# Folded transforms, the order of z's and the rows' transposes, and a split write of the output, in a fused convolution, attention and expert kernel

## The chip, the cores and the metric

The kernel runs on one core of a Trainium2 chip. The metric is the device time of one execution in microseconds (us). Before the change it was 386.15 us in the median of three runs (382.89 to 387.73).

## What is computed

The input x is 16 images of 128 channels and 16 x 16 pixels, float32. Three blocks follow each other, each with a residual sum.

```python
x = x + conv(group_norm(x))            # filters made from x itself, 7 x 7, per image and channel
t = to_tokens(x)                       # 256 tokens of 128 channels an image
q = tanh(layer_norm(t))
t = t + softmax(q q^T / sqrt(128)) layer_norm(t)
t = t + experts(layer_norm(t))         # 8 experts, hidden width 256, the best 2 of each token
```

The filters of the first block: keys are a 1 x 1 product of x to 49 channels, a softmax over the 256 pixels, a product with x (`fraw`), a 1 x 1 product, a normalisation over all 128 x 49 values, a weighting, relu, and another 1 x 1 product (`filt`). The depthwise convolution with them is done in frequency space: a real Fourier transform of side 19 (181 frequencies) written as matrix products.

## The kernel before

Two images are a pair, and there are 8 pairs. A loop of 14 rounds, unrolled in the program text, runs 7 stages over the pairs: in round i stage N works on pair i (group norm), A on pair i-1 (transposes of the normed image, keys, softmax, `fraw`), B on pair i-2 (filters, forward transform), C on pair i-3 (product of spectra, inverse transform, sum `t1`, layer norm to z), D on pair i-4 (transposes of z, tanh, scores, attention, sum `t2`, second layer norm), E on pair i-5 (normed rows, router, ranks) and F on pair i-6 (dispatch of the rows to DRAM). Round i thus has stage N up to round 7, A in rounds 1 to 8, B in 2 to 9, C in 3 to 10, D in 4 to 11, E in 5 to 12, F in 6 to 13. Beside it the weights of one expert are prepared in each of rounds 1 to 6, 11 and 12. The order of the instructions on each engine is the order in which this loop is written out; each engine runs its own list, and semaphores tie the lists together.

What the change touches, by engine and with the lines of the program before:

- TensorE, forward transform (`features_spectrum`, L833): the 256 pixels are two chunks of 128, and each of three result tiles (121 real parts, 121 imaginary parts, 124 rows with the rest of both) is a sum over both chunks: 6 products of 256 columns a pair. A float32 product shows as two records in the trace. Inverse transform (L978): for each of two chunks of pixels a sum over 4 tiles, 8 products. Filter transform (L914): 4 products whose stationary operand has 49 rows (`tapf[0:KK]`). Ranks of the tokens within their experts (L989 to L992): 14 products of 8 columns in bfloat16.
- TensorE, order within a round: filter transform, mean of the filters (L922), forward transform, transposes of z (L867), then the transposes of the normed rows (`router_input`, L844), the scores (L944), the router (L856). In rounds 10 and 11, which have no stage B, the scores come ahead of `router_input`. The transposes of the image, of z and of the rows all go to one bank, `bank_t`. ScalarE copies that bank out: to `gt`, to `qt` with tanh (L492), and to `z2t` (L453). The copy to `z2t` stands ahead of the four exponentials of the scores where stage B runs and behind them where it does not.
- VectorE: softmax's product (`kprob`, L676), the sum `t1` of the convolution in one operation of 512 columns (L746), the normed image `gbuf` (L772), which TensorE transposes at the start of the next round (L890).
- GpSimd: the powers for the reciprocal roots (L423, L429, L433, L437) and the 8 dispatches of a pair (L410), indirect DMAs of 128 rows each, half ahead of the power of L423 and half behind it.

After the rounds comes the expert phase (72 blocks of 128 rows), and then the output: SyncE loads both experts' results of a pair, VectorE adds them (L1279, L1281), and ScalarE's queue writes the pair's 256 KB to the output.

## Time and profile before

| | before |
|---|---|
| median of three runs | 386.15 us |
| profiled execution, its own time | 386.41 us |
| its span | 384.6 us |
| TensorE products busy | 302.8 us (79%) |
| VectorE busy | 236.7 us (62%) |
| GpSimd busy | 164.2 us (43%) |
| ScalarE busy | 132.4 us (34%) |
| rounds, then expert phase, then output | to 243, to 361, to 384.6 us |

The span is the stretch between the first and the last event of one profiled execution; its time is 1.8 us more. Busy shares are means over stages with different limits. TensorE (PE in the rows) has a clock of 1.2 or 2.4 GHz; the rows give the granted share of the full clock in a stretch. PEld is the load of the stationary operand, which lies beside the products.

### The profile page before, as it was taken

How to read it: one execution, taken by the hardware profiler on the slowest of the kernel's cores; microseconds unless marked ns; L12 is line 12 of the kernel's file. 1: busy time of each engine (PE TensorE's matmuls, PEld its weight loads, DVE VectorE, ACT ScalarE, POOL GpSimd, SP SyncE). 2: the span in 40 equal slices, each digit the busy share in tenths (PEclk: the TensorE clock that was granted, in tenths of full speed). 3: DMA queues.
4: the chain of work that ended last, by engine and by line, in shares of the span. 5: the costliest groups of instructions: out<-in, count | busy, mean ns of one | idle time of the engine just before them, and what ended most of it. 6: DMA issues, size and time to landing. Idle time of an engine off the chain costs nothing.

```text
span 384.6 us, 7449 instructions
## 1 busy us (share of the span) xinstructions
PE 302.8 (79%) x1731; PEld 239.7 (62%) x1732; DVE 236.7 (62%) x1006; ACT 132.4 (34%) x443; POOL 164.2 (43%) x187
## 2 busy tenths in 40 slices
PE   1686989998989899998876661599999999999200
PEld 1264667786868777777664440388878787888100
DVE  2433475488887877676866652266666676666164
ACT  0312221425152515141303012266656565666000
POOL 3000010030256565555455577046656566666400
PEclk9958896999999999989887655599999999999755
DMA  7722241221523000101010013223332322231197
GB/s 221 250 80 67 84 125 28 85 68 30 182 79 97 31 30 21 38 21 37 22 35 29 29 56 107 55 80 81 85 94 84 89 77 83 80 93 59 48 322 288
DMA packets 29945, 33.37 MB, mean 87 GB/s; under 512 B 5096, under 2 KB 23740, under 8 KB 29658
## 3 DMA queue, kind: packets, MB, share of 16 engines
q1 hardware_dynamic: 23312, 22.00, 18.9%
q0 software_dynamic: 4384, 8.60, 6.7%
q10 hardware_dynamic: 2218, 2.42, 1.8%
q8 instruction: 12, 0.20, 0.2%
q14 instruction: 19, 0.16, 0.1%
HBM read 21.76 MB, written 11.75 MB: 87 GB/s over the span
## 4 chain that ended last, share of the span: by engine, by line
PE 44%; issue 21%; POOL 21%; DMA 5%; DVE 4%; SPq 3%; ACT 1%; POOLq 0%; DVEq 0%; ACTq 0%
POOL rows_dram L410 15%; PE bank L1324 8%; PE bank L1312 5%; PE bank L1307 5%; PE bank L1308 5%; PE bank L1317 4%; PE bank L833 3%; DMA w_high<-moe_dram 2%; PE bank L876 2%; POOL ln_rstd L437 2%; PE bank L1302 2%; SPq L1160 2%; PE bank L978 2%; POOL ln_rstd L433 2%; PE bank L914 1%
## 5 line engine op out<-in xcount | busy, mean ns | idle before, releaser
L1132 POOL DMA_INDIRECT moe_dram<-ys,xs x72 | 70.4, 978 | 51.2 <-issue 30.8
L410 POOL DMA_INDIRECT rows_dram<-row,slot x64 | 62.7, 979 | 18.2 <-issue 18.2
L1324 PE MATMUL bank<-w_all,gatedt 128*128 x288 | 44.1, 276 | 0.2 <-ACT gatedt L1175 0.2
L1249 DVE SCALAR_TENSOR_TENSOR ys<-b_all,xs,bank 128x128 f32<-128x128 f32 x72 | 25.0, 347 | 28.5 <-issue 27.0
L1259 DVE SCALAR_TENSOR_TENSOR gated<-bank,xs,silu 128x256 f32<-128x256 f32 x72 | 34.8, 483 | 10.2 <-ACT silu L1183 7.8
L1183 ACT ACTIVATE silu<-bank 128x256 f32<-128x256 f32 x72 | 27.6, 383 | 35.7 <-PE bank L1312 35.7
L1324 PEld LDWEIGHTS bank<-w_all,gatedt 128*128 128x128 f32 x288 | 38.0, 192 | 0.4 <-issue 0.4
L1307 PE MATMUL bank<-w_high,x_high 128*128 x72 | 35.6, 494 | 0.0
L978 PE MATMUL bank<-zhat,const 121*128 121x256 f32 (+1 forms) x128 | 31.2, 399 | 0.0
L1312 PE MATMUL bank<-w_high,x_low 128*128 x72 | 30.3, 421 | 0.7 <-issue 0.7
L423 POOL TENSOR_TENSOR frstd<-fvar,minus_half 128x2 f32<-128x2 f32 x8 | 5.7, 708 | 57.5 <-DVE fvar L703 57.5
L1302 PE MATMUL bank<-const,xs 128*128 128x128 f32 x72 | 20.3, 282 | 11.7 <-DMA xs<-rows_dram 11.7
L1308 PE MATMUL bank<-w_low,x_high 128*128 x72 | 29.2, 405 | 0.0
L833 PE MATMUL bank<-gt,const 128*121 128x256 f32 (+1 forms) x96 | 28.4, 456 | 0.0
L1317 PE MATMUL bank<-const,gated 128*128 128x128 f32 x144 | 27.9, 276 | 0.3 <-DVE gated L1259 0.3
L1175 ACT ACTIVATE gatedt<-bank 128x256 f32<-128x256 f32 x72 | 27.3, 379 | 0.9 <-PE bank L1317 0.8
L1238 DVE TENSOR_TENSOR x_low<-bank,x_high 128x128 fp32r<-128x128 f32 x72 | 20.4, 283 | 11.6 <-ACT x_high L1171 11.1
L978 PEld LDWEIGHTS bank<-zhat,const 121*128 121x128 f32 (+1 forms) x128 | 24.8, 199 | 3.5
L1317 PEld LDWEIGHTS bank<-const,gated 128*128 128x128 f32 x144 | 20.3, 142 | 9.1 <-DVE gated L1259 0.9
L1171 ACT ACTIVATE x_high<-bank 128x128 fp32r<-128x128 f32 x72 | 19.9, 277 | 14.1 <-PE bank L1302 6.4
L833 PEld LDWEIGHTS bank<-gt,const 128*121 128x121 f32 (+1 forms) x96 | 21.0, 227 | 4.1
L437 POOL TENSOR_TENSOR ln_rstd<-ln_var,minus_half 128x4 f32<-128x4 f32 x8 | 8.4, 1056 | 30.9 <-DVE ln_var L560 30.9
(172 smaller groups left out, 593.7 us busy)
## 6 DMA issues: line engine op xcount, KB each, us to landing
xs<-rows_dram SPq DMA_DIRECT2D x72, 66.0 KB, 1.8
xc<-in_x SPq DMA_DIRECT2D x8, 256.0 KB, 2.9
wgv<-in_wg SPq DMA_DIRECT2D x8, 256.0 KB, 2.9
wgv<-in_wv SPq DMA_DIRECT2D x8, 256.0 KB, 3.4
xt<-in_xt SPq DMA_DIRECT2D x4, 512.0 KB, 4.6
xt<-moe_dram SPq DMA_DIRECT2D x8, 256.0 KB, 6.0
w_high<-moe_dram SPq DMA_DIRECT2D x8, 256.0 KB, 6.6
out<-w_high ACTq DMA_DIRECT2D x8, 256.0 KB, 5.6
```

The lines of the kernel that those rows point to most:

```text
L410: pool.indirect_dma_start(rows_dram, bass.IndirectOffsetOnAxis(ap=slot[:, f % 2, 2 * t + k:2 * t + k + 1], axis=0), row[:, f % 2, t, k, :] ...
L833: last = pe.matmul(bank_s[r // 2][0:tile_rows[r], r % 2 * 2 * C:(r % 2 + 1) * 2 * C], fwd[:, h, tile_cols[r]], gt[:, b % 2, h, :], start=( ...
L978: last = pe.matmul(bank_o[:, h * 2 * C:(h + 1) * 2 * C], inv[0:tile_rows[r], r, h * P:(h + 1) * P], zhat[0:tile_rows[r], r, :], start=(r = ...
L1132: pool.indirect_dma_start(moe_dram, bass.IndirectOffsetOnAxis(ap=xs[:, u, C + 1:C + 2].bitcast(U32), axis=0), ys[:, u, :], None, bounds_ch ...
L1183: act.activation(silu[:, u % 2, :], bank_h[u % 2][:, 0:HID], ACT.Silu).then_inc(S["silu_done"], 1)
L1259: dve.scalar_tensor_tensor(gated[:, u % 2, :], bank_h[u % 2][:, HID:2 * HID], xs[:, u, C:C + 1], silu[:, u % 2, :], ALU.mult, ALU.mult).th ...
L1302: pe.transpose(bank_x[u % 2][:, 0:P], xs[:, u, 0:C], ident).then_inc(S["xt_psum"], 1)
L1307: pe.matmul(bank_h[u % 2][:, :], x_high[:, u % 2, :], w_high[:, bass.ds(e * (2 * HID), 2 * HID)], start=True, stop=False)
L1308: pe.matmul(bank_h[u % 2][:, :], x_high[:, u % 2, :], w_low[:, bass.ds(e * (2 * HID), 2 * HID)], start=False, stop=False)
L1312: pe.matmul(bank_h[u % 2][:, :], x_low[:, u % 2, :], w_high[:, bass.ds(e * (2 * HID), 2 * HID)], start=False, stop=True).then_inc(S["h_psu ...
L1317: last = pe.transpose(bank_g[v][:, h * P:(h + 1) * P], gated[:, v, h * P:(h + 1) * P], ident)
L1324: last = pe.matmul(bank_y[v][:, 0:C], gatedt[:, v, h * P:(h + 1) * P], w2_all[:, bass.ds(e * (2 * C) + h * C, C)], start=(h == 0), stop=(h ...
```

## The change

It rests on a symmetry: with the origin in the middle of the image, pixel n and pixel 255-n have the same cosine and opposite sines. So the real parts need only the sum of the two, and the imaginary parts only the difference.

- VectorE makes sums and differences: `gfold` of the normed image (two operations of 256 columns a pair), `kfold` of the key softmax (two of 128 columns, with a factor 0.5 put into `kprob`). `gt` and `pt` then hold sum and difference in place of the two chunks.
- The forward transform is 4 products a pair (6 before), the inverse 4 (8 before). `t1` is made in three operations in place of one: one over 512 columns, which waits for the inverse, then after a wait on itself a sum and a difference of 256 columns each.
- The residual input of the upper half of the pixels has to come in reverse order: GpSimd gathers it, one indirect DMA of 128 rows of 1 KB at the start of each of rounds 1 to 8. In the same way it writes half of the output at the end with 8 indirect DMAs; ScalarE's queue writes the other half.
- The filter transform uses all 128 rows of the array; `filt` is padded with zeros.
- In rounds 4 to 9 z is transposed ahead of the filters' mean and the forward transform, and its tanh stands on ScalarE ahead of the copies of the spectrum.
- From round 9 on the transposes of the normed rows go to `bank_k` (the keys' bank), and in rounds 10 and 11 they are issued ahead of the scores.
- The ranks take 5 products in place of 14. The constants are smaller by 360 KB.

```diff
                     for r in tiles:
-                        for h in range(CHUNKS):
+                        parts = ((r, r),) if r < 2 else ((2, 0), (3, 1))
+                        for q, h in parts:
                             last = pe.matmul(bank_s[r // 2][0:tile_rows[r], r % 2 * 2 * C:(r % 2 + 1) * 2 * C],
-                                             fwd[:, h, tile_cols[r]], gt[:, b % 2, h, :],
-                                             start=(h == 0), stop=(h == CHUNKS - 1))
+                                             fwd[:, tile_cols[q]], gt[:, b % 2, h, :],
+                                             start=(q == parts[0][0]), stop=(q == parts[-1][0]))
...
                     pe.wait_ge(z2_done, e + 1)
-                    after(pe, gt_done, through(i, A))
-                    after(pe, qt_done, through(i, D))
+                    if i < rounds_of_a:
+                        after(pe, gt_done, through(i, A))
+                        after(pe, qt_done, through(i, D))
+                    else:
+                        pe.wait_ge(fraw_done, PAIRS)
+                        after(pe, z2t_done, through(i - 1, E))
...
-                                             tapf[0:KK, tile_cols[r]], filt[:, :, :].rearrange("k s c -> k (s c)"),
+                                             tapf[:, tile_cols[r]], filt[:, :, :].rearrange("k s c -> k (s c)"),
...
+                    if d is not None and b is not None:
+
+                        features_of_z(i, d)
                     if b is not None:
 
                         pe.wait_ge(f0_done, b + 1)
...
-                    if d is not None:
+                    if d is not None and b is None:
                         features_of_z(i, d)
-                    if e is not None and b is not None:
+                    if e is not None and (b is not None or a is None):
                         router_input(i, e)
...
                         for h in range(CHUNKS):
-                            for r in range(4):
-                                last = pe.matmul(bank_o[:, h * 2 * C:(h + 1) * 2 * C], inv[0:tile_rows[r], r, h * P:(h + 1) * P],
-                                                 zhat[0:tile_rows[r], r, :], start=(r == 0), stop=(r == 3))
+                            for r in (h, h + 2):
+                                last = pe.matmul(bank_o[:, h * 2 * C:(h + 1) * 2 * C], inv[0:tile_rows[r], r, :],
+                                                 zhat[0:tile_rows[r], r, :], start=(r < 2), stop=(r >= 2))
...
+                        dve.tensor_scalar(kprob[:, :], kexp[:, :], krec[:, 0:1], 0.5, ALU.mult, ALU.mult).then_inc(kprob_done, 1)
+                        dve.wait_ge(kprob_done, a + 1)
                         after(dve, pt_psum, a)
-                        dve.tensor_scalar(kprob[:, :], kexp[:, :], krec[:, 0:1], None, ALU.mult).then_inc(kprob_done, 1)
+                        dve.tensor_tensor(kfold[:, 0, :], kprob[:, 0:P], kprob[:, HW - 1:P - 1:-1], ALU.add)
+                        dve.tensor_tensor(kfold[:, 1, :], kprob[:, 0:P], kprob[:, HW - 1:P - 1:-1], ALU.subtract).then_inc(kfold_done, 1)
...
-                        dve.tensor_tensor(t1[:, c % 2, :, :].rearrange("p t c -> p (t c)"), bank_o[:, :],
-                                          xt[:, c, :, :].rearrange("p t c -> p (t c)"), ALU.add).then_inc(t1_done, 1)
+                        dve.wait_ge(ld_xm[c % 2], 16 * (c // 2 + 1))
+                        halves = t1[:, c % 2, :, :].rearrange("p (h s) c -> p h (s c)", h=CHUNKS)
+                        dve.tensor_tensor(halves, spread(bank_o[:, 0:2 * C], 1, CHUNKS),
+                                          xt[:, c, :, :].rearrange("p (h s) c -> p h (s c)", h=CHUNKS), ALU.add).then_inc(t1_step, 1)
+                        dve.wait_ge(t1_step, c + 1)
+                        dve.tensor_tensor(halves[:, 0, :], halves[:, 0, :], bank_o[:, 2 * C:4 * C], ALU.add)
+                        dve.tensor_tensor(halves[:, 1, :], halves[:, 1, :], bank_o[:, 2 * C:4 * C], ALU.subtract).then_inc(t1_done, 1)
...
                         last.then_inc(g_done, 1)
+                        dve.wait_ge(g_done, n + 1)
+                        after(dve, gt_psum, n)
+                        near = gbuf[:, n % 2, :].rearrange("p (s n) -> p s n", s=2)[:, :, 0:P]
+                        far = gbuf[:, n % 2, :].rearrange("p (s n) -> p s n", s=2)[:, :, HW - 1:P - 1:-1]
+                        dve.tensor_tensor(gfold[:, 0, :, :], near, far, ALU.add)
+                        dve.tensor_tensor(gfold[:, 1, :, :], near, far, ALU.subtract).then_inc(gfold_done, 1)
...
                     n, a, b, c, d, e, f = stages(i)
+                    if a is not None:
+
+                        after(pool, ld_xm[a % 2], 16 * (a // 2))
+                        pool.indirect_dma_start(xt[:, a, 2:4, :].rearrange("p s c -> p (s c)"), None, mirror_rows,
+                                                bass.IndirectOffsetOnAxis(ap=mirror[:, a:a + 1], axis=0)).then_inc(ld_xm[a % 2], 16)
...
         over_blocks(pool, send)
+        out_rows = out.rearrange("p b (h s) c -> (p b h) (s c)", h=CHUNKS)
+        for p in range(PAIRS):
+            pool.wait_ge(S["sum_done"], p + 1)
+            pool.indirect_dma_start(out_rows, bass.IndirectOffsetOnAxis(ap=mirror[:, p:p + 1], axis=0),
+                                    y_second[:, p, 2:4, :].rearrange("p s c -> p (s c)"), None).then_inc(S["pool_sent"], 16)
```

How this stands on two engines. First TensorE in round 10 before, from the transposes of z (L867) over the scores (L944) and the rows' transposes (L844) to the router (L856) and the inverse transform (L978):

```order
L867 MATMUL bank1<-const,z 128x128 x3
L944 MATMUL bank4<-qt 128x256 [waits e_done,ghat_done,qt_done]
L944 MATMUL bank4<-qt 128x256
L944 MATMUL bank5<-qt 128x256 x2
L844 MATMUL bank1<-const,row 128x128 [waits qt_done,gt_done,z2_done]
L844 MATMUL bank1<-const,row 128x128 x3
L856 MATMUL bank2<-router_d,z2t 128x8 [waits filt_done,pos_done,fcen_done,z2t_done]
L856 MATMUL bank2<-router_d,z2t 128x8 x3
L978 MATMUL bank3<-zhat,const 128x256 [waits t1_done,t2_done,zhat_done]
L978 MATMUL bank3<-zhat,const 128x256 x7
```

The same place in the changed program (z's transposes are L912 there, the rows' L889, the scores L992, the router L901, the inverse L1023):

```order
L912 MATMUL bank1<-const,z 128x128 x3
L889 MATMUL bank0<-const,row 128x128 [waits z2t_done,fraw_done,z2_done]
L889 MATMUL bank0<-const,row 128x128 x3
L992 MATMUL bank4<-qt 128x256 [waits e_done,ghat_done,qt_done]
L992 MATMUL bank4<-qt 128x256
L992 MATMUL bank5<-qt 128x256 x2
L901 MATMUL bank2<-router_d,z2t 128x8 [waits filt_done,pos_done,fcen_done,z2t_done]
L901 MATMUL bank2<-router_d,z2t 128x8 x3
L1023 MATMUL bank3<-zhat,const 128x256 [waits t1_done,t2_done,zhat_done]
L1023 MATMUL bank3<-zhat,const 128x256 x3
```

The rows' transposes, which wait for `z2_done`, now stand ahead of the scores, and the inverse has 4 products in place of 8.

Then VectorE in the middle of a full round before, from the relu of the filters (L740) to the sum `t1` (L746) and the ranks (L752, L753):

```order
L732 SCALAR_TENSOR_TENSOR fln<-flw,frstd,small 128x49 x2
L737 TENSOR_TENSOR row<-lexp,lrec 128x8
L740 TENSOR_SCALAR frelu<-fln 128x98
L746 TENSOR_TENSOR t<-bank,xt 128x512
L752 TENSOR_TENSOR base<-base,bank 128x8
L753 TENSOR_TENSOR pos<-bank,base 128x32
```

And in the changed program, on from the same relu (L769) to the normed image (L805) and its folds (L813, L814); rows that are as before are left out by the marks:

```order
L769 TENSOR_SCALAR frelu<-fln 128x98
L777 TENSOR_TENSOR t<-bank,xt 128x512
L780 TENSOR_TENSOR t<-t,bank 128x256
L781 TENSOR_TENSOR t<-t,bank 128x256
L786 TENSOR_TENSOR base<-base,bank 128x8
...
L805 TENSOR_SCALAR gbuf<-xc,gn_mean,gn_rstd 128x256 x2
L813 TENSOR_TENSOR gfold<-gbuf 128x256
L814 TENSOR_TENSOR gfold<-gbuf 128x256
L818 RECIPROCAL arec<-asum 128x4
```

Two operations more behind `t1`'s first, and two between `gbuf` and the rest of the round.

## Rows read from the trace of the kernel before

**Rows 1.** Windows by round: stretch, length, engines' busy us, granted clock, DMA share, GB/s.

```profile
57.80:80.00 22.20, 21.45 (x100) 16.61 (x100) 12.05 (x49) 6.66 (x25) 2.91 (x4) 0.85 0.21 66
...
122.60:142.90 20.30, 18.38 (x122) 15.42 (x122) 16.03 (x88) 6.99 (x27) 10.93 (x12) 1.00 0.09 29
...
162.00:182.00 20.00, 17.71 (x103) 14.50 (x100) 13.72 (x75) 5.50 (x22) 11.03 (x12) 0.91 0.08 28
182.00:200.00 18.00, 15.35 (x78) 12.07 (x78) 12.93 (x69) 3.51 (x12) 9.98 (x11) 0.81 0.10 34
200.00:219.00 19.00, 12.17 (x58) 9.08 (x58) 11.75 (x68) 3.62 (x12) 10.15 (x11) 0.73 0.09 30
```

**Rows 2.** Waits in round 6 (101.4 to 122.6): total us, times, longest.

```profile
DVE t L746 <- PE bank L978: 0.8, 1, 0.8
...
DVE logits L671 <- PE bank L856: 0.8, 1, 0.8
...
DVE filt L789 <- PE bank L1022: 0.4, 1, 0.4
```

**Rows 3.** The chain that ended last: start, us, what.

```profile
218.57 1.04 POOL ln_rstd L437
...
237.63 0.96 POOL rows_dram L410
...
381.39 0.69 DVE w_high L1281
```

**Rows 4.** Timeline of round 7: start, us, engine, line, operation, idle before it.

```profile
126.31 2.83 PE L833 MATMUL bank<-gt,const 128*121 128x256 f32 x12
...
130.67 0.42 DVE L599 TENSOR_TENSOR zhat<-prod 121x256 f32<-121x256 f32 x1
...
131.01 0.41 DVE L600 TENSOR_TENSOR zhat<-prod 121x256 f32<-121x256 f32 x1
...
135.57 3.71 PE L978 MATMUL bank<-zhat,const 121*128 121x256 f32 x16
...
141.51 0.73 POOL L429 TENSOR_TENSOR gn_rstd<-gn_var,minus_half 128x2 f32<-128x2 f32 x1
...
142.27 0.73 DVE L772 TENSOR_SCALAR gbuf<-xc,gn_mean,gn_rstd 128x256 f32<-128x256 f32 x2 [0.37 <-POOL gn_rstd L429]
```

**Rows 5.** Waits in round 8 (142.9 to 162).

```profile
POOL frstd L423 <- DVE fvar L703: 2.8, 1, 2.8
...
DVE logits L671 <- PE bank L856: 1.5, 1, 1.5
```

**Rows 6.** Timeline of TensorE in rounds 2 and 4.

```profile
26.59 5.46 PE L833 MATMUL bank<-gt,const 128*121 128x256 f32 x12
...
63.47 4.26 PE L833 MATMUL bank<-gt,const 128*121 128x256 f32 x12
...
68.86 1.99 PE L944 MATMUL bank<-qt 128*128 128x256 f32 x8 [0.69 <-ACT qt L492]
```

**Rows 7.** Waits in round 9 (162 to 182).

```profile
DVE logits L671 <- PE bank L856: 2.5, 1, 2.5
```

**Rows 8.** Timeline of round 10.

```profile
185.68 3.65 PE L944 MATMUL bank<-qt 128*128 128x256 f32 x8 [0.69 <-ACT qt L492]
...
187.76 1.20 DVE L635 TENSOR_SCALAR row<-t,ln_mv,ln_rstd 128x127 f32<-128x127 f32 x4 [1.12 <-POOL ln_rstd L437]
...
190.75 1.06 PE L856 MATMUL bank<-router_d,z2t 128*128 128x8 f32 x8 [0.95 <-ACT z2t L453]
...
191.66 5.39 PE L978 MATMUL bank<-zhat,const 121*128 121x256 f32 x16
```

**Rows 9.** Timeline of round 11.

```profile
205.81 1.20 DVE L635 TENSOR_SCALAR row<-t,ln_mv,ln_rstd 128x127 f32<-128x127 f32 x4 [0.90 <-POOL ln_rstd L437]
...
208.41 1.06 PE L856 MATMUL bank<-router_d,z2t 128*128 128x8 f32 x8 [0.69 <-ACT z2t L453]
```

**Rows 10.** DMA issues: queue, count, median us from issue to landing.

```profile
rows_dram<-row,slot POOLq DMA_INDIRECT x64, 2.3
```

## What I expect, and how it is worked out

> **What bounds the kernel now.** I read the windows by round first, then the waits of VectorE, then the timeline of one full round, then the timeline of the last rounds, and last the chain that ended last. A round here is one turn of the unrolled loop over the seven stages. Rounds 5 to 8 do all the work, rounds 1 to 4 fill the pipeline, rounds 9 to 13 drain it.
>
> In a full round (122.6 to 142.9 us) TensorE is busy 18.38 of 20.3 us at full clock and VectorE 16.03 [rows 1]. TensorE is the tighter one, but not by much. VectorE's idle time there is mostly waiting for TensorE: in round 6 it waits 0.8 us for the inverse transform, 0.8 for the logits, 0.4 for the filters [rows 2]. So a cheaper TensorE takes those 2.0 us away and no more; after that VectorE's own row of work is the bound. In rounds 4 and 9 the granted clock fell for a while (0.85 and 0.91 in the mean) and in rounds 10 and 11 it is 0.81 and 0.73 [rows 1]: there TensorE's chain through the router sets the pace. Behind round 11 GpSimd is the bound: from the ln2_rstd at 218.57 us it sends 16 dispatches at about 1.26 us each, the last but one at 237.63 us [rows 3], and the expert phase starts when they have landed. Nothing in the change touches the expert phase.
>
> **The change part by part, TensorE.** The forward transform has 12 records in 2.83 us, 8 afterwards: -0.94 us. The inverse has 16 in 3.71 us, 8 afterwards: -1.85 us [rows 4]. The ranks go from 14 tiny products to 5, some 0.2 us. The filter transform now uses all 128 rows of the array in place of 49. The trace has no such pair; the inverse with 121 rows costs 3.71/16 = 0.23 us a record at 256 columns, as the forward one does with 128 rows (2.83/12 = 0.24), so I take nothing, with 0.3 us a pair as the upper end. The Trainium skill (TensorE: Matmul & The Clock Gate, Part 2) says that the load of the stationary operand goes by its columns and not its rows, which would also be nothing. With z's tanh ahead of the spectrum's copies the 0.8 us wait for qt goes too (0.69 in round 4 [rows 6]). Together about 3.7 us less TensorE per full round.
>
> **VectorE.** A 256-column operation takes 0.42 us but the next one starts 0.34 us later [rows 4]. gfold: two of these and a semaphore wait on its own gbuf (0.08): +0.75. t1: two more of these and a wait on itself: +0.8. kfold: two of 128 columns, about half the step each, and a wait: +0.45. In sum +2.0 us of VectorE per full round, against the 2.0 us of waits that go away [rows 2]. **Rounds 5 and 6: 0 and +0.2.** This is the core of the forecast: what TensorE saves, VectorE spends. If the reversed reads ran at half speed, gfold and kfold would cost 1.1 us more a round; if the added work found idle places, the gain could be up to the whole 2.0.
>
> **Round 7** is held by GpSimd: gn_rstd starts at 141.51 us straight behind eight dispatches, and gbuf follows at 142.27 [rows 4]. What sets those dispatches is fvar, which comes 0.6 earlier by the logits and 0.45 later by kfold. gfold then stands behind gbuf: **+0.4**. **Round 8** has no gbuf; kfold and t1 cost 1.3; the 1.5 us wait for the logits [rows 5] and a wait for the inverse like round 6's 0.8 go: **-1.0**. GpSimd's new gather (one more 1.26 us issue at a round's start) lies in the time in which it waits for fvar, 2.8 us in round 8 [rows 5]; without that cover it would cost 1.3 us a round.
>
> **Rounds 1 to 4.** gfold stands between gbuf and the first transposes: in round 1 +0.8, and kfold and the next gfold add +1.2 before the transposes of round 2. In round 2 the forward transform runs at half clock, 5.46 us, and a third of it goes: -1.8 [rows 6]; gfold again +0.65. Round 3: -0.9 (forward), -1.0 (VectorE's wait for the inverse), +0.8 (t1), +0.75 (gfold): -0.3. Round 4: the forward transform takes 4.26 us, a third is 1.4; the wait for qt 0.69 [rows 6]; the inverse gives only the 0.8 that VectorE waits; t1 +0.8, and gfold is half hidden behind the attention product: -1.7. **Sum of rounds 1 to 4: +2.0 -1.15 -0.3 -1.7 = -1.15.**
>
> **Round 9.** VectorE waits 2.5 us for the logits [rows 7]; the forward transform is shorter, z is already through: **-1.7**.
>
> **Rounds 10 and 11 are where I expect the loss.** Before, TensorE does the scores while VectorE still normalises the rows: scores 185.68 to 189.33, rows ready at 188.96, router at 190.75 [rows 8]. The new order puts the rows' transposes ahead of the scores. TensorE then stands still until 189.0, and the scores, 3.65 us at the lower clock, run from 189.65 to 193.3. ScalarE copies z2t only after its four exponentials (its order is not changed in these rounds), so z2t is ready at 194.6 and the inverse starts at 195.65 instead of 191.66: +4.0. Being half as long (2.7 for 5.39 us) it ends 1.3 later, and t1 adds 0.8: **+2.1**. In round 11 there is no inverse to make up for it: rows ready at 207.0, scores 207.75 to 211.2, z2t 212.4, router 212.5 instead of 208.41 [rows 9]: **+3.9** after the 0.2 that the ranks give. That delay goes into ln2_rstd of the last pair, from which GpSimd's 16 dispatches run [rows 3], and no slack is behind it. If TensorE were at full clock there, the scores would take 1.9 us: round 10 would gain 1 us and round 11 lose 2.2.
>
> **The end.** Half of the output goes by GpSimd. For the last pair the issue costs about 0.96 us [rows 3] and the landing 2.3 us [rows 10]; the last sum starts at 381.39 [rows 3] and ends 382.08, so it lands at about 385.4 with the span at 384.6 us: **+1.1**, between 0 and +3 (eight indirect writes of 1 KB rows beside loads that already fill the queues).
>
> **Sum.** -1.15 + 0 + 0.2 + 0.4 - 1.0 - 1.7 + 2.1 + 3.9 + 1.1 = +3.85 us on the profiled execution's 386.4 us, which stands at the median of 386.15. I forecast 390 us, within 2% of before; 2% is about what a measurement of this kernel can tell from no change, so the borders are 378.4 and 393.9 us.
>
> **Rivals.** (A) This sum, 385 to 395 us, chance 0.45.
>
> (B) The end rounds do not lose: TensorE, now with a full array in the filter transform, keeps its clock, scores take 1.9 us, and the same term of round 4 (4.26 us against 2.83) is saved. For it: the stretches at half clock in rounds 4 and 9 follow the narrow product closely. Against it: TensorE waits longer than before in both end rounds. 390 - 6 = 384 us, chance 0.2.
>
> (C) The change does all it can: TensorE stays the bound in rounds 5 to 8, the folds lie in VectorE's idle 4 us. Then about 2 us a round come off on top of (B), so 384 - 8 = 376 us, faster. Against it: t1 and gfold stand in series on the path from the inverse to the next round's transposes. Chance 0.12.
>
> (D) The other side: TensorE's clock falls in the full rounds. After the change TensorE is busy some 15 of 20 us and idles in pieces of 1 to 2 us, for gn_mv, gfold and t1. Round 4 shows what a fall costs: the forward transform 4.26 us instead of 2.83, and the filter transform as much again, some 3 us. Two such falls ahead of the router's chain make 396 us; one and a half decide it. The Trainium skill (TensorE: Matmul & The Clock Gate, HAM oscillation) says that an engine whose idling comes between bursts falls back to its lower clock; by it (D) is the likelier. Rows 1 speak on both sides: round 7 idles 1.9 us and keeps 1.00, round 9 idles 2.3 us and has 0.91. Chance 0.23, slower.
>
> **Numbers.** Faster 0.12 (C), slower 0.26 (D and a little of A), within 2% 0.62. The range: (A) with (B) and most of (D) is 381 to 398 us; it leaves out (C).
>
> **What the new profile would show.** Right: VectorE busy some 18 us of each full round and its waits for the inverse and the logits gone; in rounds 10 and 11 TensorE idle ahead of the rows' transposes for 2 to 4 us and the scores behind them; the last dispatch but one near 240 us in place of 237.63. Wrong: full rounds of 19 us or less; a clock of 1.00 through rounds 3 to 10; a forward and inverse transform that did not shrink; or a last output that waits for GpSimd more than 3 us.

## The result: 399.76 us, and the profile after

The changed kernel takes 399.76 us in the median (399.1 to 403.89), beside 382.89 us for the kernel before in the same runs (381.81 to 387.73). The ratio is 1.0443, with a 95% interval of 1.036 to 1.0525: slower, and above both ranges that the prediction names (378.4 to 393.9 and 381 to 398 us). Every ratio here and below leaves out executions more than 1.5% above the shortest of their kernel, so it can differ from the quotient of the medians that stand beside it. The profiled execution took 403.89 us with a span of 402.1 us, 17.5 us more than the span of 384.6 us before. The other four executions of the changed kernel were 4.1 to 4.8 us shorter, at a mean granted clock of 0.844 to 0.845 where this one had 0.833. So the terms below describe its longest execution, and add up to a little more than the medians differ by.

The first section of the page of the changed kernel, engine by engine:

```profile
PE 288.1 (72%) x1563; PEld 228.1 (57%) x1564; DVE 251.8 (63%) x1055; ACT 132.9 (33%) x443; POOL 182.4 (45%) x205
```

TensorE has 14.7 us less work than before (302.8), although part of it ran at half clock; VectorE has 15.1 us more (236.7).

The best ruler through the rounds is the start of ln2_rstd on GpSimd, the last step before a pair's rows can be normalised. It exists in every round from 4 on, in either kernel, one record each. The table has the distance from one to the next, so each entry from round 5 on is one round's length. The last two columns are experiments told below, which add useless products in rounds 7 to 9 to hold TensorE's clock up (j5 and j1; j5 has some in rounds 11 and 12 too).

| round | before | after | difference | predicted | changed kernel with useless products (j5) | four products only with useless products (j1) |
|---|---|---|---|---|---|---|
| up to 4 | 84.28 | 85.00 | +0.7 | -1.15 | 86.77 | 84.34 |
| 5 | 21.36 | 20.94 | -0.4 | 0 | 20.94 | 19.14 |
| 6 | 21.20 | 21.08 | -0.1 | +0.2 | 21.08 | 19.55 |
| 7 | 20.54 | 22.98 | +2.4 | +0.4 | 20.90 | 19.62 |
| 8 | 19.40 | 18.90 | -0.5 | -1.0 | 19.82 | 18.60 |
| 9 | 19.94 | 21.91 | +2.0 | -1.7 | 18.15 | 18.01 |
| 10 | 17.86 | 20.32 | +2.5 | +2.1 | 20.84 | 16.13 |
| 11 | 13.99 | 17.83 | +3.8 | +3.9 | 17.59 | 13.99 |
| to the last sum's end | 163.5 | 164.4 | +0.8 | 0 | | |
| to the span's end | 2.5 | 8.8 | +6.3 | +1.1 | | |

The differences add up to 17.5 us. Four entries carry the miss: the end (5.2 more than predicted), round 9 (3.7), round 7 (2.0) and rounds 1 to 4 (1.9).

These are single profiles, and the experiments below show how far they carry. Up to round 9 two of them (e4, j2) run the very program of the kernel before, and two (e1, e2) that of the changed kernel. The same distances in these profiles:

| round | before, e4, j2 | changed, e1, e2 |
|---|---|---|
| up to 4 | 84.28, 86.01, 87.14 | 85.00, 85.44, 86.61 |
| 5 | 21.36, 21.35, 21.36 | 20.94, 20.93, 20.94 |
| 6 | 21.20, 21.21, 21.21 | 21.08, 21.10, 21.10 |
| 7 | 20.54, 22.22, 23.81 | 22.98, 23.00, 22.87 |
| 8 | 19.40, 19.39, 19.40 | 18.90, 19.42, 19.56 |
| 9 | 19.94, 19.89, 18.27 | 21.91, 18.04, 18.03 |

Rounds 5 and 6 are firm. The loss of round 9 is there in one profile of three, the kernel before loses round 7 too in two of three, and rounds 1 to 4 differ less between the kernels than within either.

**Rounds 5 and 6.** The windows of the changed kernel, columns as in [rows 1] (busy time of TensorE, of its weight loads, of VectorE, ScalarE and GpSimd); the first two are round 5 and round 6, then round 7, 9 and 10:

```profile
81.00:102.00 21.00, 17.39 (x107) 13.82 (x107) 19.59 (x100) 7.80 (x28) 4.79 (x5) 1.00 0.12 39
102.00:123.10 21.10, 17.33 (x108) 13.75 (x107) 19.70 (x101) 7.81 (x28) 12.64 (x13) 1.00 0.43 151
123.10:146.00 22.90, 20.29 (x103) 16.96 (x102) 18.08 (x97) 7.11 (x27) 12.41 (x13) 0.78 0.09 30
...
165.00:185.00 20.00, 16.02 (x70) 13.67 (x69) 13.94 (x74) 5.50 (x22) 11.05 (x12) 0.69 0.08 27
185.00:207.00 22.00, 14.47 (x70) 11.50 (x68) 13.71 (x71) 3.51 (x12) 9.58 (x11) 0.82 0.08 25
```

In rounds 5 and 6 VectorE is busy 19.6 of 21 us and TensorE 17.4: the bound has moved, the length has not. In round 7 TensorE is busy 20.3 us, but at a granted clock of 0.78 in place of 1.00 [rows 1], and in round 9 it is 0.69 in place of 0.91. The timeline of VectorE in round 6 has the added operations:

```profile
112.50 0.31 DVE L704 TENSOR_TENSOR kfold<-kprob 128x128 f32<-128x128 f32 x1
112.73 0.28 DVE L705 TENSOR_TENSOR kfold<-kprob 128x128 f32<-128x128 f32 x1
...
117.90 0.69 DVE L777 TENSOR_TENSOR t<-bank,xt 128x512 f32<-128x512 f32 x1
118.63 0.42 DVE L780 TENSOR_TENSOR t<-t,bank 128x256 f32<-128x256 f32 x1
118.97 0.41 DVE L781 TENSOR_TENSOR t<-t,bank 128x256 f32<-128x256 f32 x1
...
122.01 0.42 DVE L813 TENSOR_TENSOR gfold<-gbuf 128x256 f32<-128x256 f32 x1
122.35 0.42 DVE L814 TENSOR_TENSOR gfold<-gbuf 128x256 f32<-128x256 f32 x1
```

A 256-column operation is 0.42 us and the next one starts 0.34 us after it (its step), a 128-column one about 0.3 with a step of 0.23, and a reversed read costs no more than a plain one. These are the durations that were forecast.

**Where the clock fell.** Three windows of 3 us of round 7 in the changed kernel, and two of round 9:

```profile
132.00:135.00 3.00, 1.27 (x9) 0.89 (x8) 2.93 (x23) 0.59 (x5) 1.94 (x2) 1.00 0.17 59
135.00:138.00 3.00, 2.84 (x8) 2.39 (x9) 1.99 (x18) 0.48 (x2) 1.92 (x3) 0.50 0.03 8
138.00:141.00 3.00, 3.00 (x17) 2.54 (x16) 1.56 (x6) 0.00 (x0) 2.39 (x3) 0.50 0.20 68
...
168.00:171.00 3.00, 1.08 (x5) 0.58 (x4) 1.98 (x12) 1.43 (x6) 1.92 (x2) 1.00 0.00 0
...
177.00:180.00 3.00, 3.00 (x8) 2.37 (x9) 1.96 (x18) 0.23 (x1) 1.74 (x2) 0.50 0.00 0
```

Ahead of the fall TensorE had been busy 1.27 of 3 us, waiting in pieces for the logits, kfold and gn_mv; ahead of the second, 1.08 of 3, with one wait of 2.11 us for the rows. The waits ahead of the first fall, in brackets:

```profile
133.17 0.35 PE L1001 MATMUL bank<-fsqs,const 128*128 128x2 f32 x2 [0.69 <-DVE logits L696]
133.95 0.44 PE L1008 MATMUL bank<-const,kfold 128*128 128x128 f32 x2 [0.42 <-DVE kfold L705]
135.16 0.58 PE L1014 MATMUL bank<-gn_mv,const 128*128 128x2 f32 x2 [0.77 <-DVE gn_mv L721]
```

Then the inverse transform and the attention product of round 7 run at 1.2 GHz:

```profile
135.61 3.76 PE L1023 MATMUL bank<-zhat,const 121*128 121x256 f32 x8
...
141.51 3.73 PE L1059 MATMUL bank<-z,e_attn 128*128 128x128 f32 x16
```

The halved inverse, 8 records, takes 3.76 us, as long as the full one of 16 records before [rows 4]. In e1, the same program up to there, the clock fell in round 7, and the second time late in round 8 (0.77 from 160 to 165 us) and not in round 9, where the inverse took 1.98 us:

```profile
175.95 1.98 PE L1023 MATMUL bank<-zhat,const 121*128 121x256 f32 x8
```

**Rounds 10 and 11** went as forecast. TensorE in round 10 of the changed kernel, to be read against [rows 8]:

```profile
193.10 1.12 PE L889 MATMUL bank<-const,row 128*128 128x128 f32 x4 [3.55 <-DVE row L660]
194.01 3.08 PE L992 MATMUL bank<-qt 128*128 128x256 f32 x8
198.51 1.06 PE L901 MATMUL bank<-router_d,z2t 128*128 128x8 f32 x8 [1.42 <-ACT z2t L477]
199.42 3.38 PE L1023 MATMUL bank<-zhat,const 121*128 121x256 f32 x8
```

TensorE stands still for 3.55 us for the rows, the scores follow them, and the router waits another 1.42 us for z2t. In round 11 the waits are 4.46 and 1.42 us.

**The end.** The queue records of the block's end, the kernel before first, then the changed one: duration in ns (least, median and most of one record, so three times the same), and the start in us. A drain is the record with which an engine's program closes.

```profile
L336 POOLq DRAIN  x1: 8705/8705/8705, 359.4 to 359.4; - x1
```

```profile
L350 POOLq DRAIN  x1: 8472/8472/8472, 393.4 to 393.4; - x1
...
L350 SPq DRAIN  x1: 7/7/7, 396.3 to 396.3; - x1
```

GpSimd closes its program with a drain of 8.5 to 8.7 us. Before, it began at 359.4 us, when GpSimd had sent its last block, and lay wholly under the output. Now GpSimd has to issue the last write of the output (393.59 us), and its drain begins with it, at 393.4 us, and ends at 401.9 us; SyncE is through at 396.3 us, 5.6 us ahead of that. The windows show that no transfer is under way any more:

```profile
394.00:396.00 2.00, 0.00 (x0) 0.00 (x0) 0.00 (x0) 0.00 (x0) 0.56 (x1) 0.50 0.38 131
396.00:398.00 2.00, 0.00 (x0) 0.00 (x0) 0.00 (x0) 0.00 (x0) 0.00 (x0) 0.50 0.00 0
```

### The profile page after: what moved, and what is told of

The parts are those of the page before. It is cut to its first block, busy times and chain, and to the rows that moved or that the text cites. A ratio compares the mean times of both kernels' runs of the same rounds, so it can differ in the third digit from the quotient of the medians.

```text
span 402.1 us, 7194 instructions
## 1 busy us (share of the span) xinstructions
PE 288.1 (72%) x1563; PEld 228.1 (57%) x1564; DVE 251.8 (63%) x1055; ACT 132.9 (33%) x443; POOL 182.4 (45%) x205
## 4 chain that ended last, share of the span: by engine, by line
PE 37%; issue 23%; POOL 22%; DVE 7%; DMA 5%; SPq 2%; ACT 2%; POOLq 0%; DVEq 0%; ACTq 0%
POOL rows_dram L428 15%; PE bank L1376 8%; PE bank L1364 5%; PE bank L1359 4%; PE bank L1360 4%; PE bank L1369 4%; POOL ln_rstd L461 2%; PE bank L1354 2%; DMA w_high<-moe_dram 2%; PE bank L874 2%; SPq L1211 2%; POOL ln_rstd L457 2%; PE bank L921 1%; PE bank L959 1%; PE bank L935 1%
## 5 line engine op out<-in xcount | busy, mean ns | idle before, releaser
L1354 PE MATMUL bank<-const,xs 128*128 128x128 f32 x72 | 20.3, 282 | 11.9 <-DMA xs<-rows_dram 11.9
L1059 PE MATMUL bank<-z,e_attn 128*128 128x128 f32 x128 | 22.9, 352 | 7.0 <-issue 5.8
L1369 PEld LDWEIGHTS bank<-const,gated 128*128 128x128 f32 x144 | 20.3, 142 | 9.2 <-DVE gated L1311 0.9
L1059 PEld LDWEIGHTS bank<-z,e_attn 128*128 128x128 f32 x128 | 21.2, 259 | 7.5 <-issue 7.5
L1023 PE MATMUL bank<-zhat,const 121*128 121x256 f32 (+1 forms) x64 | 20.7, 480 | 0.0
L453 POOL TENSOR_TENSOR gn_rstd<-gn_var,minus_half 128x2 f32<-128x2 f32 x8 | 5.7, 717 | 31.1 <-DVE gn_var L791 31.1
```

What stands on the lines that cost most here:

```text
L1059: last = pe.matmul(bank_o[:, (h * 2 + s) * C:(h * 2 + s + 1) * C], e_attn[:, s, k, h * P:(h + 1) * P], z[:, d % 2, k * 2 + s, :], start=(k ...
L1354: pe.transpose(bank_x[u % 2][:, 0:P], xs[:, u, 0:C], ident).then_inc(S["xt_psum"], 1)
L1369: last = pe.transpose(bank_g[v][:, h * P:(h + 1) * P], gated[:, v, h * P:(h + 1) * P], ident)
```

## The experiments

Every ratio is to the kernel before on the same chip, and times of different chips are not compared. Ratios of different groups are compared in places, and that is weaker: one kernel that ran on two chips (e3 and h1) stands at 1.0085 and 0.9887. So differences of that size between groups are called shown only where the profiles' rounds show them. e1 to e4 ran together (the kernel before 386.12 us there, 382.42 to 392.89), f1 to f4 (before 418.07 us, the expert phase being slower on that chip), h1, h2, g1 and g2 (414.45 us), j1, j2, j3 and j5 (385.31 us), j4 and k2 (385.47 us; one execution of the kernel before took 1605.93 us there). The starts of ln2_rstd lie ahead of the expert phase.

### The end and the order: four kernels

**e1: the whole output by ScalarE's queue**, in the changed kernel; the host lays out the reversed half.

```diff
-    act.dma_start(out[:, p, 0:2], y_second[:, p, 0:2, :])
-    pool.indirect_dma_start(out_rows, mirror, y_second[:, p, 2:4, :])   # and its wait
+    act.dma_start(out[:, p], y_second[:, p, :, :])
```

> The changed kernel with its output written as before: whole pairs by ScalarE's queue; the layout of the output array holds the reversed half, and the host puts it in order. Theory (the end): in the changed kernel GpSimd's drain of 8.5 us starts only behind its last output write and holds the program's end 6 us after the last data moved; without those writes the drain lies under the output again, so 6 us less, about 394 us. Rival (the loss is all in the rounds, the end only looks idle): 1 us less, 399 us.

Measured: 394.53 us, ratio 1.0302 (1.027 to 1.0333), 0.0141 or 5.4 us below the changed kernel's ratio, which was measured in another group. The drain is under the output again, and the span ends 2.4 us behind the last sum in place of 8.8:

```profile
L350 POOLq DRAIN  x1: 8732/8732/8732, 367.5 to 367.5; - x1
```

**e4: the kernel before, where GpSimd waits for the last sum at its end** and issues nothing more.

```diff
         over_blocks(pool, send)
+        pool.wait_ge(S["sum_done"], PAIRS)
```

> The kernel before with one wait more: GpSimd waits for the last output sum before it ends, and issues nothing there. Theory A (the drain at GpSimd's end is a fixed cost of ending, whatever was issued): it starts at the last sum and ends 8.5 us later, so 6 us longer, 389 us. Theory B (the drain takes long because it comes close behind indirect DMAs; here it comes 20 us later): no change, 383 us.

Measured: 394.77 us, ratio 1.032 (1.0273 to 1.0367), for one wait that does no work. The closing records:

```profile
L336 POOLq DRAIN  x1: 6609/6609/6609, 385.8 to 385.8; - x1
...
L336 SPq DRAIN  x1: 7/7/7, 387.8 to 387.8; - x1
```

SyncE is through at 387.8 us, and the span ends at 392.6 us, when the drain is over: 4.8 us, where it is 0.2 us before. So the drain belongs to the ending of GpSimd's program, whether it wrote just before or not, and is free where another engine works 9 us longer. The medians differ by 8.65 us, though, and the ratio comes to 12 us. In the profile the rest lies in rounds whose program is unchanged: ln2_rstd of round 11 stands at 222.86 us in place of 218.57, with round 7 1.7 us longer and the filter transform of round 3 at the lower clock, where the kernel before had 1.99 us:

```profile
43.41 3.77 PE L914 MATMUL bank<-filt,const 49*121 49x256 f32 x8
```

Why all four executions were that long stays open.

**e2: the scores ahead of the rows' transposes in rounds 10 and 11**, as before, in the changed kernel.

```diff
-    if e is not None and (b is not None or a is None):
+    if e is not None and b is not None:
         router_input(i, e)
     ... scores ...
+    if e is not None and b is None:
+        router_input(i, e)
```

> The changed kernel with the scores ahead of the rows' transposes again in rounds 10 and 11, nothing else. Theory (the order at the end rounds costs what the prediction's steps for rounds 10 and 11 say): router in round 11 some 4 us earlier, 5 to 7 us less in all, about 394 us. Rival (the lower clock there, not the order, makes the loss): 0 to 2 us less, 398 to 400 us.

Measured: 395.34 us, ratio 1.0308 (1.022 to 1.0396), 5.2 us below the changed kernel by the ratios, again of two groups. In the profiles rounds 10 and 11 take 16.85 and 13.77 us in place of 20.32 and 17.83, 7.5 us less; they had lost 6.3 us in the table.

**e3: both, and the input's reversed half laid out by the host too**, without the gather of rounds 1 to 8.

```diff
-    sp.dma_start(xt[:, pairs, 0:2], a_in["xt"][:, pairs, 0:2])
-    pool.indirect_dma_start(xt[:, a, 2:4], mirror_rows, mirror)
+    sp.dma_start(xt[:, pairs], a_in["xt"][:, pairs])
```

> Both of these, and the residual input reversed by its layout in DRAM, so that GpSimd has no gather in rounds 1 to 8. Theory (the two costs add, the gather is hidden): 12 us less than the changed kernel, 388 us, still above the kernel before because of the clock in rounds 7 and 9. Rival (the gather delays GpSimd's dispatches): 383 us or less.

Measured: 387.24 us, ratio 1.0085 (1.0045 to 1.0124). On this one chip e1 and e3 differ by the order and the gather: 2.2% or 8.3 us, and rounds 10 and 11 of their profiles by 7.7 us. e2 and e3 differ by the end and the gather: 2.2% or 8.5 us, and the stretch behind the last sum by 6.3 us. The gather was not tried alone, but the rounds price it: round 5 lasts 20.93 to 20.94 us in the four profiles with it (changed, e1, e2, j5) and 20.82 to 20.83 us in six without (e3, f3, f4, h1, h2, j3), and round 6 21.08 to 21.10 us with it and 21.07 to 21.11 us in those of e3, h1, h2 and j3. So it costs 0.1 us a round or less. What is left, the folded transforms themselves, gains nothing on this chip (the same kernel is 1.1% faster on another, h1 below). The rest of the study is on that.

### What the folds cost and what the products give: three kernels

**f1: only TensorE's saving.** The kernel before with four products each way; the other terms are left out, and nothing is folded.

```diff
-    for h in range(CHUNKS):          # forward, 6 products
+    for h in ((r,) if r < 2 else (0, 1)):
...
-    for r in range(4):               # inverse, 8 products
+    for r in (h, h + 2):
```

> The kernel before with 4 forward and 4 inverse products a pair; the other 2 and 4 are left out, and so are their terms of the sums. No folds. Theory (TensorE bounds the full rounds, so its 2.8 us a round are worth nearly all): 8 rounds of 2 us or more, 370 us or less. Rival (VectorE is next, only its waits of 2.0 us a full round can go, less in the ends): 374 to 378 us.

Measured: ratio 1.0035 (0.9991 to 1.008). Twelve records fewer a pair (4 forward, 8 inverse), and no gain at all. Two windows of it, in round 7 and in rounds 8 to 9:

```profile
135.00:147.00 12.00, 12.00 (x70) 10.01 (x69) 7.45 (x39) 1.53 (x6) 4.54 (x5) 0.70 0.07 24
147.00:159.00 12.00, 9.69 (x63) 8.29 (x62) 8.99 (x51) 5.47 (x21) 7.25 (x8) 0.86 0.09 29
```

The clock fell five times between 131 and 219 us, and this is no matter of one profile: f1's ten executions had mean granted clocks of 0.824 to 0.846, the 26 of the kernel before beside them 0.857 to 0.890. Its round 5 is 19.14 us long (21.36 before), its round 7 23.77 (20.54).

**f2: only VectorE's part.** The kernel before with all six fold operations, into tiles that nothing reads, and t1's reader waiting for them.

```diff
+    dve.tensor_tensor(kfold[:, 0, :], kprob[:, 0:P], kprob[:, HW - 1:P - 1:-1], ALU.add)
+    dve.tensor_tensor(kfold[:, 1, :], kprob[:, 0:P], kprob[:, HW - 1:P - 1:-1], ALU.subtract)
...  # the same for gfold (256 columns), and two of 256 columns behind t1
```

> The kernel before with the folds' six VectorE operations added, into tiles that nothing reads, in series as in the changed kernel (TensorE's transposes wait for gfold and kfold, the attention for the third operation on t1). TensorE's work is as before. Theory (they stand in series and VectorE has no free place for them): 8 rounds of 1.5 to 2 us, 396 to 400 us. Rival (they fall into VectorE's waits for TensorE): 2 to 4 us more, 388 us.

Measured: ratio 1.0475 (1.033 to 1.0621), 20 us. That is more than the forecast's 2.0 us in each of 8 rounds. That the folds stand in series with a TensorE that has no slack is argued and not shown: the profile is of an execution 10.9 us above the shortest, and round 5, at full clock, is only 1.2 us longer there (22.58 us).

**f3: e3 with z's transposes and tanh at their old place.**

```diff
-    if d is not None and b is not None:
-        features_of_z(i, d)          # ahead of the filters' mean
     ... forward transform ...
-    if d is not None and b is None:
+    if d is not None:
         features_of_z(i, d)
```

> The changed kernel with plain output and input and the scores first (387.2 us), and z's transposes and tanh back at their old places, behind the forward transform and behind the copies of the spectrum. Theory (z ahead saves the wait for qt, 0.7 us in each of rounds 4 to 9, part of which VectorE's bound hides): 1 to 3 us more, 389 us. Rival (z ahead empties TensorE where the clock then falls, in rounds 7 and 9): 0 to 3 us less, 385 us.

Measured: 1.0033 (0.9982 to 1.0085), beside 1.0003 (0.9962 to 1.0044) for e3 with useless products, which ran with it. Moving z's transposes is worth nothing that can be told, though the comparison has the useless products in it too. Round 5 is 20.83 us in both.

### Does the clock take TensorE's saving back

In these kernels two useless products of 512 columns stand in each of rounds 7, 8 and 9, at the place where the expert's weights stand in rounds 2 to 6. Nothing reads them.

```diff
+    if i in (7, 8, 9):
+        for h in range(2):
+            pe.matmul(bank_d0[:, :], ident, const[:, 0:512], start=True, stop=True)
```

**f4: e3 with them.**

> The same 387.2 us kernel with two useless products of 512 columns (1.9 us at full clock) in each of rounds 7, 8 and 9, at the place where rounds 2 to 6 prepare an expert's weights; nothing reads them. Theory (TensorE's clock falls in rounds 7 and 9 because it has too little to do there): the clock stays at 1.00 from 125 to 165 us and the kernel gets 2 to 4 us faster, 384 us. Rival (TensorE's time still counts, the fall has another cause): 2 to 4 us slower, 390 us.

Measured: 1.0003 (0.9962 to 1.0044). Its clock was 1.00 from 153 to 192 us, but 0.50 from 147 to 150 us, where the theory had 1.00 from 125 us on. e3 itself was not in that group, so both were run again side by side.

> The changed kernel with the whole output on ScalarE's queue, the reversed half of the input laid out by the host (no gather, no scatter, no GpSimd writes at the end), and the scores ahead of the rows' transposes in rounds 10 and 11. It is run beside the next three kernels as their common base. Expected: ratio to before 1.000 to 1.012, as the same kernel gave 1.0085 on another chip; granted clock below 0.8 for several microseconds in rounds 7 and 9.

> The base with two useless products of 512 columns in each of rounds 7, 8 and 9 (some 0.9 us of TensorE a round), which nothing reads. Clock theory: the fall in rounds 7 and 9 is what costs there, so the clock stays at 1.00 from 123 to 186 us and the time is 2 to 4 us below the base. VectorE theory: the clock costs nothing because VectorE is the bound, the time is that of the base or up to 1 us above it.

Measured: h1, without them, 0.9887 (0.9849 to 0.9926); h2, with them, 0.9921 (0.9884 to 0.9958). In the profiles ln2_rstd of round 11 stands at 222.38 and 219.87 us, 2.5 us earlier with the useless work (rounds 7 to 9 together 59.39 us in place of 60.40), but the times do not show it: the medians lean the other way, 411.20 us with it and 409.37 without. By the times this pair speaks for no gain. The base itself, at 1.0085 on one chip and 0.9887 on another, differs by more than either interval.

**j1: f1 with them**, the plainest test, since f1 has TensorE's saving alone (the same terms are left out). It ran on another chip than f1.

> The kernel before with only the four products each way (terms left out, no folds) and two useless 512-column products in each of rounds 7, 8 and 9. Without the useless ones it gave 1.0035 (0.9991 to 1.008), its clock fell four times between 132 and 219 us, and ln2_rstd of round 6, ahead of the falls, was 3.5 us earlier than before. Clock theory (the chip takes TensorE's saving back by clocking down once TensorE idles more): the clock is 1.00 from 123 to 190 us, ln2_rstd of round 9 is near 183 us (186.7 before, 185.9 without filler), ratio 0.985 to 0.995. Rival (GpSimd's eight dispatches a round set rounds 7 to 9): clock held, ln2_rstd of round 9 at 185 to 187 us, ratio 1.00 to 1.005.

Measured: 378.84 us, ratio 0.9794 (0.966 to 0.9928), where f1 had 1.0035. All windows of rounds 7 to 9 have the full clock:

```profile
135.00:147.00 12.00, 10.30 (x64) 8.11 (x63) 9.79 (x46) 4.89 (x17) 6.85 (x8) 1.00 0.08 27
147.00:159.00 12.00, 11.07 (x78) 8.98 (x77) 8.66 (x55) 3.14 (x16) 7.03 (x8) 1.00 0.11 36
```

ln2_rstd of round 9 came at 179.26 us, 6.6 us ahead of f1. Rounds 7 to 9 take 56.2 us in place of 62.5, with 1.8 us of useless work in each: that much the clock had cost. The 2.4% between the ratios is more than this, of two chips, and holds another 7.6 us of rounds 6, 10 and 11, where no useless product stands (round 6, 1.6 us of them, at a clock of 1.00 in both). Beside the kernel before on its own chip j1 is 2.1% faster, by three executions. The rival, GpSimd's dispatches as the bound of rounds 7 to 9, falls.

**j5: the changed kernel itself with them**, and with more of them at the heads of rounds 11 and 12 (three and four) and one ahead of the ranks of each.

> The changed kernel as it is, with all these useless products. It was 1.044 (1.036 to 1.0525). Clock theory: rounds 7 and 9 give back 2.5 to 4 us and rounds 11 and 12 give 3, so 1.025 to 1.032; what stays is the end by GpSimd (6 us) and the order in rounds 10 and 11. Rival: rounds 7 and 9 are late for VectorE's folds or the gather and not for the clock, and ratio stays at 1.038 to 1.05.

Measured: 399.26 us, ratio 1.0346 (1.0251 to 1.0441). By the ratios 3.7 us better than the changed kernel, with intervals that overlap and of two groups; the rounds (sixth column of the table) say more. Round 7 takes 20.90 us in place of 22.98. Round 9 takes 18.15 in place of 21.91, 1.8 us less than before, as predicted for round 9 (-1.7); but e1 and e2 have 18.04 and 18.03 us there without a useless product, so this can't be put down to them. The inverse transform of round 9, first in the changed kernel, then here:

```profile
176.77 3.76 PE L1023 MATMUL bank<-zhat,const 121*128 121x256 f32 x8
```

```profile
177.36 1.90 PE L1036 MATMUL bank<-zhat,const 121*128 121x256 f32 x8
```

Rounds 10 and 11 did not get shorter: there the order sets the time.

Round 7 is where all 20 profiles can be set side by side. The eight with useless products in rounds 7 to 9 have 19.6 to 20.9 us there. Of the twelve without, ten have 22.1 us or more, and only the kernel before (20.54) and g1 (20.95) have less. So the useless products do take the loss out of round 7. They do not hold the clock throughout: in j5 it was 0.83 from 145 to 155 us, and round 8 is 0.3 to 0.9 us longer there than in the three profiles of the changed program without them.

**j2: the kernel before with useless products in rounds 11 and 12 only.**

```diff
+    if i in (11, 12):
+        useless(3 if i == 11 else 4)     # 512 columns each, into bank_k
...
+    if i in (11, 12):
+        useless(1)                       # ahead of the ranks
```

> The kernel before with useless 512-column products where TensorE waits in rounds 11 and 12 (three at round 11's head, four at round 12's, one ahead of the ranks of each). The scores (3.45 us) and the attention product (3.76 us) of round 11 run at half clock before. Clock theory: both take 1.9 to 2.0 us, ln2_rstd of round 11 comes 3 to 3.5 us earlier (215 in place of 218.6) and the kernel is 3 to 4 us faster, ratio 0.990 to 0.993. Rival (the clock does not come back by some products ahead, or the useless ones delay z's transposes by 1 us): 0.998 to 1.003.

Measured: ratio 1.0021 (0.9971 to 1.0072). The scores did run at full clock, the attention product did not:

```profile
208.04 1.99 PE L952 MATMUL bank<-qt 128*128 128x256 f32 x8 [0.69 <-ACT qt L492]
...
211.51 0.66 PE L844 MATMUL bank<-const,row 128*128 128x128 f32 x4 [1.47 <-DVE row L635]
...
216.94 3.48 PE L1024 MATMUL bank<-z,e_attn 128*128 128x128 f32 x16
```

With the scores 1.5 us shorter TensorE waits 1.47 us for the rows: in round 11 they were the next thing late, and only the wait has moved. This profile is of an execution of 390.75 us, where the shortest took 383.22. In it the clock fell in round 7 as well (0.72 from 135 to 147 us), in a kernel whose round 7 was unchanged, and so it did in e4 (profiled at 394.44 us, the shortest 394.36). So the fall hangs by little before the change too; the kernel before ranges from 382.03 to 392.27 us on that chip, and whether this is why was not tried.

**j3: e3 with all of these useless products.**

> The changed kernel with plain output and input halves and the scores first, with the useless products of rounds 7, 8, 9 and those of rounds 11 and 12. On one chip it gave 0.9887 without any and 0.9921 with those of rounds 7 to 9. Clock theory: ln2_rstd of round 11 at 216 us (219.9 with those of rounds 7 to 9 alone), 3 to 4 us below that kernel, ratio 0.98 to 0.998. Rival (nothing but GpSimd's dispatches and VectorE set these rounds): no change, 0.99 to 1.008.

Measured: 383.27 us, ratio 0.9945 (0.9894 to 0.9996). ln2_rstd of round 11 at 215.60 us, 3.0 us ahead of before, 13.4 ahead of the changed kernel and 10.4 ahead of e1.

### Does VectorE hold what is left

**g1: e3 with gfold and kfold made by TensorE**, and **g2**, the same with the useless products of rounds 7 to 9.

```diff
-    dve.tensor_tensor(gfold[:, 0, :, :], near, far, ALU.add)        # and three more
-    pe.transpose(dst, gfold[:, h, s, :], ident)
+    pe.matmul(dst, gbuf[...first half...], ident, start=True, stop=False)
+    pe.matmul(dst, gbuf[...second half...], signs[h], start=False, stop=True)
```

> The base with gfold and kfold made by TensorE: the folded transposes are two accumulating products, one against the identity and one against plus or minus the identity, and x's second half is stored reversed by the host so that no operand is read backwards. VectorE loses four operations of 0.6 us a round in sum 1.2 us and two waits on itself, TensorE gains six products of 128 columns, about 0.7 us. VectorE theory (the folds stand in series between normalisation and the next transposes and hold rounds 3 to 7): 4 to 8 us faster than the base, ratio to before 0.985 to 1.0, and the clock falls less. Clock theory: TensorE is bounded by its clock all the same, and the gain is 0 to 2 us.

> The previous kernel with the same useless products in rounds 7, 8 and 9. If the fall of the clock is still there without the folds on VectorE, the filler gives 2 to 4 us more; if the six added products already keep the clock up, it gives nothing or costs up to 1 us.

Measured, beside h1 (0.9887) and h2 (0.9921): g1 0.9931 (0.9885 to 0.9977), g2 0.9968 (0.989 to 1.0047). No gain, against the expectation. I had priced the added products like transposes. Transposes step by 0.11 us each (four from 86.59 to 87.03 us), these by 0.22 us in g1's timeline of round 5:

```profile
82.53 0.39 PE L922 MATMUL bank<-const,gbuf 128*128 128x128 f32 x2
82.75 0.39 PE L923 MATMUL bank<-const,gbuf 128*128 128x128 f32 x2
82.97 0.39 PE L922 MATMUL bank<-const,gbuf 128*128 128x128 f32 x2
...
86.59 0.60 PE L898 MATMUL bank<-const,z 128*128 128x128 f32 x4
```

Twelve products at 0.22 us in place of six transposes at 0.11 are 2.0 us more on TensorE, which was then busy 19.74 of 21 us in round 5, as much as in the kernel before.

**j4: j3 with the forward transform unfolded again**, six products from plain transposes; only the inverse stays folded.

```diff
-    dve.tensor_tensor(gfold[:, 0, :, :], near, far, ALU.add)      # gfold and kfold gone
-    for q, h in (((r, r),) if r < 2 else ((2, 0), (3, 1))):       # 4 products
+    for h in range(CHUNKS):                                       # 6 products
         pe.matmul(..., fwd[:, h, tile_cols[r]], gt[:, b % 2, h, :])
```

> The changed kernel with plain halves, the scores first and all useless products (that one gave 0.9945), and with the forward transform unfolded again: six products from plain transposes, no gfold and no kfold on VectorE; the folded inverse and t1's three operations stay. Per full round VectorE loses 1.2 us, TensorE gains 0.94. VectorE theory (the folds hold rounds 4 to 8, so they should be bought only where TensorE gives most for them: 1.85 us for 0.8 in the inverse, 0.94 for 1.2 in the forward transform): full rounds of 20.2 us in place of 20.9, ln2_rstd of round 11 at 211 to 213 us (215.6 with the forward fold), ratio 0.982 to 0.990. Rival (GpSimd's eight dispatches and its own waits set the rounds): ln2_rstd of round 11 at 215 to 217 us, ratio 0.992 to 1.0.

Measured: 377.6 us, ratio 0.9781 (0.9717 to 0.9846), on its chip: 2.2% faster than the kernel before. The 0.9945 with the forward fold (j3) is of another chip, so the rounds have to tell the forward fold's part. Round 5 is 19.86 us long and round 6 19.96, where the folded ones had 20.94 and 21.08, and both engines are near their limit:

```profile
102.00:123.00 21.00, 19.16 (x119) 15.41 (x118) 19.43 (x104) 7.74 (x29) 11.62 (x12) 1.00 0.33 120
```

ln2_rstd of round 11 stands at 211.32 us, 7.3 us ahead of before. So VectorE's folds were the bound of the full rounds, and the forward ones did not pay: 1.2 us of VectorE for 0.94 of TensorE, where the inverse's 0.8 us buy 1.85.

**k2: j4 with two more useless products in round 11**, one of 512 columns behind the scores and one of 256 ahead of the router.

> The previous kernel with a useless 512-column product behind the scores of round 11, where TensorE waits 1.7 us for the rows, and one of 256 columns ahead of its router, where it waits 0.7 us for z2t. Clock theory: the attention product of round 11 ran at half clock (3.76 us) with the useless products of the previous kernel because TensorE had idled 1.7 and 0.7 us; now 2.0 us, ln2_rstd of round 11 another 1 to 1.8 us earlier. Rival (the eight-column products of the router, not the waits, bring the clock down): no change, 0 to 0.5 us.

Measured: 0.9842 (0.9779 to 0.9906), no better than j4 in the times. In the profiles the attention product of round 11 took 2.58 us in place of 3.66 and ln2_rstd came at 209.13 us in place of 211.32. That is the expected size, and the times don't confirm it.

## Why the prediction was wrong, point by point

**Durations on both engines: right.** The forward transform went from 2.83 to 1.97 us, the inverse from 3.71 to 1.98, the folds cost what was said, the filter transform with 128 rows (L959) still takes 379 ns a record in the median, where 49 rows (L914) took 376. The reversed reads had no price.

**Rounds 5 and 6 (0 and +0.2, measured -0.4 and -0.1): right, and for the reason given.** VectorE went to 19.6 of 21 us. The table of three profiles each has it without exception, and j1 and j4 show it from the other side: without folds the rounds are 19.1 to 19.6 us, with the inverse's alone 19.9.

**Rounds 1 to 4 (-1.15, measured +0.7): not settled.** Rounds 1 and 2 went as worked out: the transposes of rounds 2 and 3 start 1.7 and 0.8 us later than before (24.24 for 22.56, 40.80 for 40.00), where +2.0 and +0.85 were forecast. Then round 4 starts 2.0 us late (59.87 for 57.86) in place of 0.55. In round 3 the filter transform ran partly at the lower clock, and TensorE waited 3.07 us for gfold where it had waited 1.36 for gbuf:

```profile
43.44 3.29 PE L959 MATMUL bank<-filt,const 128*121 128x256 f32 x8
...
59.87 1.11 PE L935 MATMUL bank<-const,gfold 128*128 128x128 f32 x4 [3.07 <-DVE gfold L814]
```

But e4, with the program of before, ran its filter transform at the lower clock there too (3.77 us), and the kernel before has 84.28 to 87.14 us up to round 4 in three profiles, the changed one 85.00 to 86.61. That this term was mis-sized can't be told from such profiles; that the gain of 1.15 us was there, neither.

**Rounds 7 and 9 (+0.4 and -1.7, measured +2.4 and +2.0): the step that failed is the choice of (A) over (D).** The sum took TensorE's saving at full clock. What happened in round 7 was rival (D), at 0.23: TensorE idles in pieces, the clock falls, and the saving is spent at 1.2 GHz, 22.9 to 23.0 us in three profiles of the changed program. With useless products (j5) round 7 comes out at +0.4, as the sum had it. In f1, with TensorE relieved and nothing else changed, every execution has a lower mean clock than any of the kernel before beside it, and the saving is gone (1.0035). So (D) holds in kind. In size it is less sure. The kernel before loses round 7 too in e4 and j2, so a part of the +2.4 is luck of its profile. And round 9's +2.0 is of one profile, of the longest execution: in e1 and e2 the second fall came in round 8 and cost less, and round 9 has 18.0 us, -1.9, close to the forecast. How much the clock costs the median execution, no profile here shows.

The Trainium skill (TensorE: Matmul & The Clock Gate, A second HAM failure mode) tells of a kernel in which small idle times between groups of products made the clock go back and forth; the waits of 0.42 to 0.77 us ahead of the fall of round 7 agree with it. The section that the prediction names, HAM oscillation, has long waits for DMAs as its case. I had read the page and weighed it down by round 7 of the kernel before, which idles 1.9 us and keeps 1.00; in two more profiles of that program round 7 does not keep it.

**Round 8 (-1.0, measured -0.5)**: right in sign in this profile only; e1 and e2, in which the second fall came late in round 8, have 19.42 and 19.56 us for 19.40 before, no gain.

**Rounds 10 and 11 (+2.1 and +3.9, measured +2.5 and +3.8): right**, mechanism and size. e1 has the same 20.32 and 17.75 us, and with the old order (e2) rounds 10 and 11 are 7.5 us shorter. One step inside was off: the scores of round 10 took 3.08 us and not 3.65.

**GpSimd's gather (priced at nothing): right.** Round 5 is 0.1 us longer with it and round 6 the same, so it is hidden under GpSimd's waits, as was said.

**The end (+1.1, measured +6.3): the other step that failed, and the largest, is what was counted.** The issue (0.97 us) and the landing were counted (2.3 us; the eight writes took 5.4 us in the median), the end of GpSimd's own program was not. Its drain stood in the trace of before, at 359.4 us and 8.7 us long, in a place where it was hidden, and I asked of the moved step only what it issues. e1 and e4 settle it: with the writes back on ScalarE's queue the span ends 2.4 us behind the last sum, and one wait on GpSimd brings 4.8 us of drain back.

The end does not explain the miss alone. e1, without it, still stands at 1.0302, some 11.6 us, where the sum without its last term had +2.75. The order is 6.3 us of that, about as forecast (6.0). Of the rest only round 7 has a cause that the runs show; where the remainder lies in an execution of median length stays open.

## What to carry to other kernels

An engine that is given new work at the end of a kernel also brings its end with it: look in the trace for the records that close each engine's program, and ask what hides them. Work taken off TensorE can be lost again to its clock, so compare the granted clock ahead of and behind the relieved stretch, in more than one profile, since the same program kept its clock in one and lost it in the next, and try a few useless products before giving a saving up. Where work is traded between two engines that are both near the bound, price each piece as a ratio and keep only the pieces that buy more than they cost: here 1.85 for 0.8 us was worth it and 0.94 for 1.2 us was not.

## What the runs showed of the hardware that I had not expected

- GpSimd's program ends with a drain of 6.6 to 8.7 us in ten profiles read for it: 7.8 to 8.7 us right behind its last DMA (nine), 6.6 us where it had only waited since its last one (e4).
- Useless products of 1.8 us a round make rounds 7 to 9 shorter, 62.5 us in f1 and 56.2 us in j1, by the clock.
- One program falls to the lower clock at a place in one profile and not in the next: round 7 of the kernel before takes 20.54, 22.22 and 23.81 us in three.
- A product against an identity matrix costs twice a transpose in float32: 0.22 us for 0.11 us at 128 columns.
- The same kernel (e3, h1) stands at 1.0085 to the kernel before on one chip and at 0.9887 on another. The reason is open, and so differences of up to 2% between ratios of different chips prove nothing by themselves.
